# Window attention: one value slot in the key product, value copies split between VectorE and ScalarE, two low parts of U behind the mean

## The reference, cut to what matters

```python
qkv = (xw @ qkv_w + qkv_b).reshape(Bw, N, 3, HEADS, dh).transpose(2, 0, 3, 1, 4)
q, k, v = (qkv[0], qkv[1], qkv[2])
attn = jnp.einsum('bhnd,bhmd->bhnm', q, k) * dh ** (-0.5)
attn = jax.nn.softmax(attn + bias, axis=-1)
out = jnp.einsum('bhnm,bhmd->bhnd', attn, v).transpose(0, 2, 1, 3).reshape(Bw, N, C)
out = out @ proj_w + proj_b
```

## Time and profile before

| | |
|---|---|
| median of 3 runs | 1960.83 us (1960.3 to 1974.0) |
| profiled execution: its own time | 1975.34 us |
| its span | 1973.7 us |
| mean granted TensorE clock | 0.951 of full |
| busy, share of the span | PE 1772.9 us (90%), ACT 1541.7 (78%), DVE 1365.0 (69%), POOL 1170.0 (59%) |

### The profile page before, as it was taken

One profiled execution on the slowest core, in us unless ns is written; L12 is line 12 of the kernel. 1 busy time (PEld: TensorE's weight loads), 2 busy tenths in 40 slices (PEclk: granted clock), 3 DMA queues, 4 the chain that ended last, 5 costly groups with the idle time before them and its releaser, 6 DMA issues. The chain is left out here.

```text
span 1973.7 us, 90330 instructions
## 1 busy us (share of the span) xinstructions
PE 1772.9 (90%) x38186; PEld 1076.4 (55%) x38186; DVE 1365.0 (69%) x2016; ACT 1541.7 (78%) x2904; POOL 1170.0 (59%) x1048
## 2 busy tenths in 40 slices
PE   4999999999999999999999998995899967999996
PEld 2666556656565565655666565651497943333332
DVE  7776666767676676766767676642777766888883
ACT  3788788888888788888888888873766647888882
POOL 5687686777778677777877777652255550122222
PEclk9999999999999899999999999996799985999998
DMA  4344554444444344444444444411488759999994
GB/s 111 94 108 99 139 129 103 105 102 110 100 113 102 96 107 100 116 99 105 106 107 103 104 112 99 98 45 43 109 216 216 214 135 170 227 253 253 262 258 147
DMA packets 233228, 262.26 MB, mean 133 GB/s; under 512 B 167079, under 2 KB 179911, under 8 KB 232711
## 3 DMA queue, kind: packets, MB, share of 16 engines
q1 hardware_dynamic: 217478, 217.50, 46.2%
q0 software_dynamic: 15360, 39.08, 6.6%
HBM read 160.82 MB, written 80.88 MB: 122 GB/s over the span
## 5 line engine op out<-in xcount | busy, mean ns | idle before, releaser
L416 POOL TENSOR_TENSOR shift<-const_b,qmax 113x588 bf16<-113x588 bf16 x256 | 299.4, 1170 | 231.8 <-DVE qmax L511 230.1
L563 DVE TENSOR_TENSOR x<-ps_m,x 112x392 f32<-112x392 f32 x128 | 66.5, 561 | 272.8 <-PE ps_m L1028 272.8
L511 DVE TENSOR_REDUCE qmax<-ps_s 113x12 f32<-113x588 f32 x256 | 194.9, 761 | 66.8 <-PE ps_s L907 66.7
L1487 POOL DMA_DIRECT2D out_rolled<-r_OUT x128 | 63.8, 503 | 270.2 <-DVE r_OUT L1587 270.2
L716 ACT ACTIVATE P<-ps_t 113x588 f32<-113x588 f32 x256 | 172.0, 672 | 58.4 <-PE ps_t L959 57.1
L748 ACT ACTIVATE G<-ps_m 128x392 f32<-128x392 f32 x384 | 178.3, 500 | 46.0 <-PE ps_m L1009 45.5
L503 DVE TENSOR_TENSOR Ul<-Uf 113x784 bf16<-113x784 f32 x192 | 208.5, 1113 | 0.0
L1333 PE MATMUL conv_ps<-xin,band_now 64*64 64x448 bf16 x2688 | 203.1, 364 | 2.2 <-DVE x_low L1228 2.2
L406 POOL TENSOR_TENSOR xhl<-xh 113x784 bf16<-113x784 f32 x64 | 200.7, 3137 | 2.2 <-DVE xh L551 2.2
L709 ACT COPY Uf<-ps_m 113x392 f32<-113x392 f32 x384 | 172.9, 486 | 33.0 <-PE ps_m L874 24.8
L1333 PE MATMUL conv_ps<-x_low,band_now 64*64 64x448 bf16 x1344 | 179.6, 351 | 0.0
(11 more groups left out here) (244 smaller groups left out, 5203.9 us busy)
## 6 DMA issues: line engine op xcount, KB each, us to landing
xin<-rows_scratch SPq DMA_DIRECT2D x96, 236.0 KB, 3.8
XT<-x_tokens SPq DMA_DIRECT2D x64, 294.0 KB, 3.3
X<-x_windows SPq DMA_DIRECT2D x128, 147.0 KB, 3.4
RS<-rs_scratch SPq DMA_DIRECT2D x128, 147.0 KB, 3.4
XR<-x_windows SPq DMA_DIRECT2D x128, 147.0 KB, 3.2
x_scratch<-x SPq DMA_DIRECT2D x128, 147.0 KB, 3.4
y_scratch<-y POOLq DMA_DIRECT2D x96, 196.0 KB, 2.9
r_RS<-rs_scratch SPq DMA_DIRECT2D x128, 147.0 KB, 4.6
```

The costliest lines, as they stand in the source:

```text
L416: nc.gpsimd.tensor_tensor(shift[:, j % 2], e, m, ALU.mult).then_inc(S["md"], 1)
L511: nc.vector.tensor_reduce(qmax[:, j % 2, :].rearrange("p (b n) -> p b n", b=2), ps_s[0:R, :, 0:2 * HQ].rearrange("p b (n t) -> p b n t", t ...
```

## The change

- UV is 4: one value slot. A matmul of `keys_and_values` moves 196 columns instead of 245. The windows of the two rows come out on partitions 0 to 48 and 64 to 112 with the values at the same columns, so V can no longer be filled by one copy: each copy is now two, one of partitions 0 to 48 and one of 64 to 112, each 49 by 192, written into V with a stride of two elements (V is set to zero once). V holds the channels of the two rows interleaved.
- The copies of quads 0, 2 and 3 move from ScalarE to VectorE (`keep_values` there, L538 in the changed file); quad 1's stays on ScalarE (two copies of 49 by 192). VectorE's copy of quad 0 waits for quad 0's exponential; ScalarE's exponentials of quads 2 and 3 wait for VectorE's copies.
- For quads 2 and 3 the two pairs of windows change places, so that one `key_ones` and one V layout serve all; `divide`, `project` and `first_residual` follow (same sizes, columns in blocks of 98, proj_w twice in the pack).
- On VectorE, `u_low` of heads 1 and 2 moves behind `subtract_mean`, the first `query_max` of the next strip, `divide` and the copy of quad 3; head 1 stands before, head 2 behind the second `query_max`.
- At setup two copies of the value weights over 784 columns take the place of eight over 392, and GpSimd's low parts of them have half the columns.

```diff
@@ -111,3 +111,3 @@
 
-        UV = HEADS + 2
+        UV = HEADS + 1
         SV = UV * TOK
...
@@ -187,6 +186,6 @@
         P = sb("P", [R, 2, QP, HEADS, TOK])
-        V = sb("V", [R, 2, QP, 2 * C])
+        V = sb("V", [R, 2, QP, C, 2])
         lden = sb("lden", [2 * C, W])
         rden = sb("rden", [2 * C, 2, W])
-        O = sb("O", [2 * C, 2, STRIP])
+        O = sb("O", [2 * C, 2, 2, QUADS, 2 * TOK])
         x1 = sb("x1", [R, 2, STRIP])
...
@@ -244,3 +243,3 @@
         names = ("t_sum t_mean t_cen t_sqr t_var t_ln t_rs xh0 lo0 uu u_hi u_lo s_q mx kb md st ex vev pv lnd rdn nrm "
-                 "proj x1_made x1_lo cen xc sq sq_lo var ln rs xh1 lo1 f1 ge f2 x2_made").split()
+                 "proj x1_made x1_lo cen xc sq sq_lo var ln rs xh1 lo1 f1 ge f2 vev_mid x2_made").split()
         S = {nm: sem(f"{nm}_done") for nm in names}
...
@@ -250,2 +249,16 @@
 
+        def of_kind(ap, a):
+            return ap.rearrange("p (j a t) -> p a j t", a=2, t=2 * TOK)[:, a]
+
+        def kept(q):
+
+            return (S["vev"], 2 * (q // 4 * 3 + (0, 1, 1, 2)[q % 4])), (S["vev_mid"], 2 * (q // 4 + (q % 4 > 1)))
+
+        def kept_values(p, j):
+
+            lo = ROWB * p
+            to = V[lo:lo + TOK, j % 2, :, :, p].rearrange("p (b k) c -> p b k c", b=2)
+            of = ps_t[lo:lo + TOK, :, 0:2 * SV].rearrange("p b (k c) -> p b k c", c=SV)[:, :, :, HQ:HQ + C]
+            return to, of
+
         def bank(use, b):
...
@@ -458,4 +471,4 @@
             for r in range(2):
-                pool.wait_ge(values_spread, 4 * r + 4)
-                nc.gpsimd.tensor_tensor(Ul[:, r, HEADS:, :], Uf[:, r, HEADS:, :], U[0][:, r, HEADS:, :], ALU.subtract
+                pool.wait_ge(values_spread, r + 1)
+                nc.gpsimd.tensor_tensor(Ul[:, r, HEADS, :], Uf[:, r, HEADS, :], U[0][:, r, HEADS, :], ALU.subtract
                                         ).then_inc(values_low, 1)
...
@@ -515,2 +528,13 @@
 
+            def keep_values(s, j):
+
+                if s.real:
+                    q = 4 * s.n + j
+                    wait(dve, S["st"], q + 1)
+                    if j == 0:
+                        wait(dve, S["ex"], q + 1)
+                    wait(dve, S["pv"], q - 1)
+                    for p in range(2):
+                        nc.vector.tensor_copy(*kept_values(p, j)).then_inc(S["vev"], 1)
+
             def divide(s, j):
...
@@ -521,3 +545,3 @@
                     wait(dve, S["proj"], 2 * (s.n - 1))
-                    nc.vector.tensor_tensor(O[:, s.slot(2), W * j:W * j + W], ps_out, rden[:, j % 2, :], ALU.mult
+                    nc.vector.tensor_tensor(O[:, s.slot(2), :, j, :], halves(ps_out), halves(rden[:, j % 2, :]), ALU.mult
                                             ).then_inc(S["nrm"], 1)
...
@@ -530,7 +554,8 @@
                     wait(dve, S["x2_made"], 2 * (s.n - 1))
-                    for b in range(2):
-                        wait(dve, S["proj"], 2 * s.n + b + 1)
+                    for a in range(2):
+                        wait(dve, S["proj"], 2 * s.n + a + 1)
                         nc.vector.scalar_tensor_tensor(
-                            out=x1[:, r, cols_of(b)], in0=bank("proj", b)[0:R, 0:HALF], scalar=out_b[:, 0:1],
-                            in1=XR[:, r, cols_of(b)], op0=ALU.add, op1=ALU.add).then_inc(S["x1_made"], 1)
+                            out=of_kind(x1[:, r, :], a), in0=bank("proj", a)[0:R, 0:HALF].rearrange("p (j t) -> p j t", j=QUADS),
+                            scalar=out_b[:, 0:1], in1=of_kind(XR[:, r, :], a), op0=ALU.add, op1=ALU.add
+                            ).then_inc(S["x1_made"], 1)
 
...
@@ -572,2 +597,3 @@
                 query_max(s, 2)
+                keep_values(s, 0)
                 token_sums(s.at(4))
...
@@ -580,9 +606,11 @@
                 divide(s, 0)
+                keep_values(s, 2)
                 u_low(nxt, 0)
-                u_low(nxt, 1)
                 subtract_mean(prv)
-                u_low(nxt, 2)
                 query_max(nxt, 0)
                 divide(s, 1)
+                keep_values(s, 3)
+                u_low(nxt, 1)
                 query_max(nxt, 1)
+                u_low(nxt, 2)
 
...
@@ -634,6 +662,3 @@
                 lo = ROWB * g
-                src_v = ps_s[lo:lo + C + 1, 1, 0:C].rearrange("p (h d) -> p h d", h=HEADS)
-                for t, at in ((wv, g), (wv_swap, 1 - g)):
-                    link(nc.vector.tensor_copy(t[lo:lo + C + 1, 0:2 * C].rearrange("p (h g d) -> p h g d", h=HEADS, g=2)[:, :, at, :],
-                                               src_v))
+                link(nc.vector.tensor_copy(wv[lo:lo + C + 1, 0:C], ps_s[lo:lo + C + 1, 1, 0:C]))
             assert chain[0] == WV_V
...
@@ -714,2 +739,4 @@
                     wait(act, S["st"], q + 1)
+                    if j >= QUADS // 2:
+                        wait(act, *kept(q + 1)[0])
                     wait(act, S["pv"], q - 1)
...
@@ -724,5 +751,4 @@
                     wait(act, S["pv"], q - 1)
-                    nc.scalar.copy(V[:, j % 2].rearrange("p (b n) c -> p b n c", b=2),
-                                   ps_t[0:R, :, 0:2 * SV].rearrange("p b (n c) -> p b n c", c=SV)[:, :, :, HQ:HQ + 2 * C]
-                                   ).then_inc(S["vev"], 1)
+                    for p in range(2):
+                        nc.scalar.copy(*kept_values(p, j)).then_inc(S["vev_mid"], 1)
 
...
@@ -756,3 +782,2 @@
                 log_variance(old, 0)
-                keep_values(s, 0)
                 invert_sums(prv, 3)
...
@@ -772,3 +797,2 @@
                 u_high(nxt, 2, 1)
-                keep_values(s, 2)
                 exp_scores(s, 2)
...
@@ -783,3 +807,2 @@
                 gelu(old, 1, 0)
-                keep_values(s, 3)
                 gelu(old, 1, 1)
...
@@ -797,8 +820,4 @@
             for r in range(2):
-                for a in range(2):
-                    for n, t in enumerate((wv, wv_swap)):
-                        nc.scalar.copy(
-                            Uf[:, r, HEADS + a, cols_of(n)].rearrange("p (w t) -> p w t", t=TOK),
-                            t[:, TOK * a:TOK * a + TOK].unsqueeze(1).to_broadcast([R, WINS // 2, TOK])
-                        ).then_inc(values_spread, 1)
+                nc.scalar.copy(Uf[:, r, HEADS, :].rearrange("p (w t) -> p w t", t=TOK),
+                               wv[:].unsqueeze(1).to_broadcast([R, WINS, TOK])).then_inc(values_spread, 1)
             steps(step, -1, N + 2)
...
@@ -905,3 +924,3 @@
                                     at = HQ * k + TOK * h
-                                    w = QP * j + 2 * b + k
+                                    w = QP * j + 2 * (b ^ j // 2) + k
                                     ins = mm(ps_s[to:to + TOK, b, at:at + TOK],
...
@@ -922,3 +941,4 @@
                     wait(pe, S["ex"], q)
-                    wait(pe, S["vev"], q)
+                    for copied in kept(q):
+                        wait(pe, *copied)
                     r = s.slot(2)
...
@@ -967,13 +987,16 @@
                     wait(pe, S["ex"], q + 1)
-                    wait(pe, S["vev"], q + 1)
+                    for copied in kept(q + 1):
+                        wait(pe, *copied)
                     wait(pe, S["nrm"], q)
                     for k in range(QP):
+                        at = TOK * (k ^ j // 2 * 2)
                         for h in range(HEADS):
                             lo = 2 * DH * h
-                            mm(ps_out[lo:lo + 2 * DH, TOK * k:TOK * k + TOK], V[:, j % 2, k, lo:lo + 2 * DH],
+                            mm(ps_out[lo:lo + 2 * DH, at:at + TOK], V[:, j % 2, k, DH * h:DH * h + DH, :],
                                P[:, j % 2, k, h, :], start=True, stop=True)
                     for b in range(2):
+                        at = 2 * TOK * (b ^ j // 2)
                         for h in range(HEADS):
                             lo = 2 * DH * h
-                            ins = mm(ps_den[lo:lo + 2 * DH, 2 * TOK * b:2 * TOK * (b + 1)], key_ones[:, b ^ j // 2, :],
+                            ins = mm(ps_den[lo:lo + 2 * DH, at:at + 2 * TOK], key_ones[:],
                                      P[:, j % 2, 2 * b:2 * b + 2, h, :], start=True, stop=True)
...
@@ -984,7 +1007,7 @@
                     wait(pe, S["nrm"], 4 * s.n + 4)
-                    for b in range(2):
-                        free_m("proj", b)
-                        mm(bank("proj", b)[0:R, 0:HALF], proj_w[:], O[:, s.slot(2), cols_of(b)],
+                    for a in range(2):
+                        free_m("proj", a)
+                        mm(bank("proj", a)[0:R, 0:HALF], proj_w[:, a, :], O[:, s.slot(2), a],
                            start=True, stop=True).then_inc(S["proj"], 1)
-                        taken("proj", b, S["x1_made"], 2 * s.n + b + 1)
+                        taken("proj", a, S["x1_made"], 2 * s.n + a + 1)
 
```

(25 more changed lines are left out.)

2 lines of the change are left out of this document (removed).

## The result

The changed kernel takes **1985.38 us** in the median of 4 runs (1982.16 to 1989.64), the kernel before beside it 1962.38 (1960.3 to 1974.0, 4 runs): ratio 1.0108, 95% interval 1.007 to 1.0146. In a later series on one chip it was 1.0103 (1.0079 to 1.0128). It is slower by 1%; forecast were 1951 us, with a range up to 1976. The profiled execution took 1984.45 us, span 1982.8.

A forecast was written before the change was run, and what follows sets the result against it. It took a loop through VectorE, GpSimd's low1 and fc1, not TensorE, as the bound: +0.32 - 0.46 = -0.14 us a strip, -8.5 us, with setup -1.5; from the 1960.83 median, 1951 us, range 1928 to 1976.

The forecast's parts named there:

- x1 to fc1: From x1 written to fc1's start: GpSimd's low1 no longer held up, fc1 at 5.11 instead of 5.57 us, -0.46 a strip.
- The mean, not low1, is late next: Before fc1: low1 ends 3.75 us after x1, the mean's first half at 5.06, so fc1 waits for the mean.
- Second residual to x1: VectorE's stretch up to x1: quad 0's pair of copies, 0.76 us, partly absorbed, delays x1 by +0.32 us a strip.
- TensorE's own work ahead of fc1 is not what is late: TensorE before fc1: its work becomes 0.49 us a strip shorter, so fc1 does not wait for it.
- Fc1 to fc2: nothing: From fc1 to fc2's end: ScalarE's moved copies and VectorE's two added pairs, 1.5 us, change nothing in the strip.
- That u_low 1 and 2 move behind the mean at no cost: VectorE before the next second residual: 3.87 us of idle time covers the late u_low and added pairs, costing nothing.
- The setup, -1.5: Setup: GpSimd's low parts shrink from 8.01 to some 3 to 4 us, mostly covered by TensorE's start; -1.5 us.
- TensorE sets the time (1): Rival for the whole loop: TensorE bounds, the full 0.49 us a strip counts, 1929 us; chance 0.17.
- Delay and relief cancel or overturn (2): Rival: copies of 0.45 to 0.5 us before x1 give +0.1 a strip, 1961 to 1967; 0.17 with the unshortened-product rival.
- The relief doesn't come (3): Rival: another chain keeps fc1 in place, the pair before x1 adds 0.32 us a strip, 1981 us; chance 0.08.
- The shared port (4): Rival: VectorE's copies take the port GpSimd shares, some +1.0 us a strip, 2022 us; chance 0.08.
- The product isn't shortened (5): Rival: weight loads limit the key product, -0.02 us a strip, 1958 us; 0.17 together with the cancel-or-overturn rival.

The follow-up runs named there:

- e2: Against the changed kernel, u_low of head 0 moved behind subtract_mean, so the mean comes first; 1964.78 us, ratio 0.9974 to the kernel before.
- e1: Against the changed kernel, quad 0's pair of value copies moved from VectorE back to ScalarE; 1955.63 us, ratio 0.991 to the kernel before.
- E4: Against the kernel before, only u_low 1 and 2 moved behind the mean, two value slots and all copies on ScalarE; 1969.49 us, ratio 1.0002.
- e7: Against the changed kernel, quad 3's pair of copies on VectorE made twice, once into a spare buffer; 1990.71 us, ratio 1.0105 to the kernel before.
- e5: Against the changed kernel, an unused second value slot put back, so key-product matmuls move 245 columns; 1993.92 us, ratio 1.0105 to the kernel before.
- e3: Against the changed kernel, quad 0's copies back on ScalarE and the mean ahead of every u_low; 1955.41 us, ratio 0.9915; repeated, 1949.2 us.

## Why the prediction was wrong

**The failed step is "x1 to fc1", -0.46 us.** It came as -0.2. "The mean, not low1, is late next" was right, and so was the chain: low1 1.49 us, u_low blocked to 0.84 behind low1 (0.83 forecast), then the mean, then fc1. The size was wrong by small pieces that all add:
- x1_low took 2.22 instead of 2.15, since normalise1 took 1.10 instead of 1.03: low1's end at 3.82 instead of 3.75.
- The mean starts at 905.47, 0.02 *behind* the u_low's end of 905.45 (0.03 in the median over the strips). I had it 0.08 before, as in the earlier trace rows at 902.19: 0.11. Its first half ends at 5.25, 5.06 forecast; the 0.57 for it was right.
- Fc1 starts 0.11 behind that, not 0.05, which was what the earlier trace rows had behind low1. The 0.11 could have been read in before: there fc1's later parts start 0.11 behind the gelu that frees their bank (median of 50). Why the two differ I did not find.

The mean's late start comes from the copies. E2 has the same pair of instructions twice in a strip, first behind the mean, which reads PSUM itself, and then directly behind a pair of copies:

```profile
893.02 1.25 DVE L516 TENSOR_TENSOR Ul<-Uf 113x784 bf16<-113x784 f32 x1
894.20 0.76 DVE L524 TENSOR_REDUCE qmax<-ps_s 113x12 f32<-113x588 f32 x1
...
895.15 0.73 DVE L538 COPY V<-ps_t 49x192 f32<-49x192 f32 x2
895.91 1.13 DVE L516 TENSOR_TENSOR Ul<-Uf 113x784 bf16<-113x784 f32 x1
897.07 0.77 DVE L524 TENSOR_REDUCE qmax<-ps_s 113x12 f32<-113x588 f32 x1
```

Both u_low end 0.83 behind a GpSimd operation, so both stood blocked. Yet the row maxima start 0.07 before the end of the first (894.27) and 0.03 behind the end of the second (897.04). The same holds in every trace: the first operation that reads PSUM behind a pair of copies starts 0.03 behind its predecessor's end even when operations on SBUF alone stand between (medians of 47 to 50 strips), and without a pair it starts some 0.08 before, unless it waits for something else. The prediction counted such a hold inside the pair and right behind it, but not this third one.

**"Second residual to x1", +0.32 us,** came as +0.37. The pair was right: 0.355 us a copy, 895.17 to 895.95 for both where I had 0.76, and t_mean at 0.17. But the divide is the first to read PSUM behind quad 0's pair, and so it starts 0.03 behind t_var's end where I took 0.08 before it: the same third hold, +0.49 at the divide. (In e1, without the pair, it starts 0.05 behind t_var's end too, but 0.55 earlier in the strip and with more scatter, so there it waits for an input.) Of that 0.09 is won back ahead of x1, where the earlier trace rows have a small gap that I hadn't seen, and 0.03 in the first residual itself. The net of the loop is +0.19 instead of -0.14: 0.33 us times 63 is 21 us, most of the miss, and the two holds of 0.11 are, by estimate, two thirds of the 0.33. As the experiments show, both terms depended on one instruction pair or one line's place: e2 changes the one by -0.43, e1 the other by -0.55.

**"TensorE's own work ahead of fc1 is not what is late"** held for after. But I compared low1 with fc1's start and never asked how far behind TensorE stood: 0.09 us, at 5.43 against 5.52. E4 shows what that means, a relief of 0.15 us whatever GpSimd gains, and e2 what the shorter product could have given. A relief of 0.46 needs both at once, low1 earlier and TensorE earlier.

**"Fc1 to fc2: nothing"** held, 7.32 against 7.29, and e7 shows the cover under quad 3's pair. **That u_low 1 and 2 move behind the mean at no cost** held in full strips and failed in the first two, where the covering work doesn't exist. **The setup, -1.5,** came as +0.8 to 1.3 at the first square. GpSimd's low parts did shrink, to the row below from the 8.01 of the earlier trace rows, and the first key product starts at 36.39 us instead of 38.33, 1.9 earlier (40.31 in e5, which has the wide low parts and after's order). The first wait of 2.97 above is larger than that gain, and the difference fits the first square; no run isolates it.

```profile
25.15 2.95 POOL L473 TENSOR_TENSOR Ul<-Uf 113x784 bf16<-113x784 f32 x2 [2.70 <-ACT Uf L821]
```

**The rivals.** TensorE sets the time (1): not in after; e2 and e3 make it so, and gain. Delay and relief cancel or overturn (2) is what came, though not by dearer copies but by the smaller relief and the late divide; I had let it end at 1967. The relief doesn't come (3), 1981 us, is nearest in time; yet it names another chain, and 0.2 of the relief came. The shared port (4): no, the copies took 0.355 beside GpSimd's work and the shift beside them 1.17. The product isn't shortened (5): groups start 0.091 us apart, as forecast. The Trainium skill ("TensorE: Matmul & The Clock Gate", LDWEIGHTS) has a load at its columns over 1.2 ns, by which four loads one after the other would be an estimate of 163 ns; the 0.091 us, like the 0.027 of the earlier trace rows, show that these four, each for its own quadrant, do not run one after the other.

**The base** was low too: with 1967 for the kernel before, my own sum would have been 1957, and the measured loss is 19 to 23 us. Of the 34 us between 1951 and 1985, 21 are thus the loop, 6 the base, and some 6 the first strips and the setup.
